# Products with the values in three batches per head pair of the first layer instead of six

## The reference, cut to what matters

```python
a1 = _attn(q, k1, v1, causal=True)
a2 = _attn(q, ks, vs, causal=False)
a3 = _attn(q, kw, vw, causal=True)
g = gate[:, :, None, None, None]
out = g[:, 0] * a1 + g[:, 1] * a2 + g[:, 2] * a3
out = out.transpose(0, 2, 1, 3).reshape(B, T, N_HEAD * V_HEAD)
return out @ w_proj
```

## Time and profile before

| | us |
|---|---|
| median of 3 runs (lowest, highest) | 3538.37 (3537.81, 3544.86) |
| the profiled execution's own time | 3538.17 |
| its span, first to last instruction | 3536.3 |
| busy: PE, PEld, DVE, ACT, POOL | 3216.3, 2335.8, 1985.7, 1558.5, 929.1 |
| mean granted clock of TensorE, share of full speed | 0.942 |
| matmuls of line 897 with the first layer's values / ones / 64 selected keys' values | 337.8 / 404.6 / 67.2 |

### The profile page before, as it was taken

One profiled execution on the slowest core, in us unless ns is written; L12 is line 12 of the kernel. 1 busy time (PEld: TensorE's weight loads), 2 busy tenths in 40 slices (PEclk: granted clock), 3 DMA queues, 4 the chain that ended last, 5 costly groups with the idle time before them and its releaser, 6 DMA issues. The chain is left out here.

```text
span 3536.3 us, 58809 instructions
## 1 busy us (share of the span) xinstructions
PE 3216.3 (91%) x20560; PEld 2335.8 (66%) x20560; DVE 1985.7 (56%) x6978; ACT 1558.5 (44%) x3441; POOL 929.1 (26%) x1840
## 2 busy tenths in 40 slices
PE   4999889997899979999889998899889997899988
PEld 3776657765677656776567765677656776577665
DVE  3665466646566465664656646566465654566545
ACT  1454345543455334553445535455253552545434
POOL 0222222222222222222222232222322223222222
PEclk8999899998899989999999998999989998999989
DMA  2000000000000000000000000100000000000000
GB/s 90 28 13 13 1 14 25 19 7 1 20 19 19 7 1 25 19 13 7 1 25 19 13 7 1 31 16 10 7 1 32 19 7 6 14 19 19 11 3 7
DMA packets 31438, 53.75 MB, mean 15 GB/s; under 512 B 3472, under 2 KB 13456, under 8 KB 30864
## 3 DMA queue, kind: packets, MB, share of 16 engines
q1 hardware_dynamic: 31120, 49.64, 4.4%
HBM read 44.91 MB, written 4.72 MB: 14 GB/s over the span
## 5 line engine op out<-in xcount | busy, mean ns | idle before, releaser
L1483 ACT ACTIVATE PR<-work 128x512 f32<-128x512 f32 (+1 forms) x1088 | 641.9, 599 | 574.6 <-PE work L860 472.3
L1125 DVE CUSTOM_DVE_ANT_0 work<-work,KEEPB 128x384 f32<-128x384 f32 (+3 forms) x1536 | 666.5, 481 | 75.9 <-PE work L821 74.6
L1609 POOL TENSOR_SCALAR_AFFINE_SELECT PR<-PR 128x256 f32<-128x256 f32 (+1 forms) x960 | 348.6, 367 | 925.9 <-ACT PR L1483 921.8
L821 PE MATMUL work<-BIG 96*128 96x448 f32 (+9 forms) x1664 | 446.2, 364 | 39.0 <-DVE NMX L1125 15.8
L1109 DVE TENSOR_TENSOR BIG<-work,BIG 96x512 fp32r<-96x512 f32 (+1 forms) x455 | 284.6, 628 | 326.9 <-ACT BIG L1378 325.9
L1599 POOL TENSOR_TENSOR TOK<-AB 128x256 f32<-128x256 f32 (+1 forms) x325 | 220.1, 677 | 850.2 <-DVE AB L1079 850.2
L858 PE MATMUL work<-BIG 99*128 99x512 f32 (+4 forms) x1152 | 404.5, 351 | 0.3
L897 PE MATMUL outs<-PR,ONES 128*32 128x512 f32 (+4 forms) x2304 | 404.6, 458 | 0.0
L821 PEld LDWEIGHTS work<-BIG 96*128 96x128 f32 (+1 forms) x1664 | 279.9, 203 | 184.1 <-issue 92.5
L859 PE MATMUL work<-BIG 96*128 96x512 f32 (+4 forms) x1152 | 382.6, 332 | 0.0
L860 PE MATMUL work<-BIG 96*128 96x512 f32 (+4 forms) x1152 | 381.7, 331 | 0.0
(11 more groups left out here) (163 smaller groups left out, 5291.6 us busy)
## 6 DMA issues: line engine op xcount, KB each, us to landing
WKW<-w_kw_dram SPq DMA_DIRECT2D x65, 256.0 KB, 2.7
WSEL<-w_sel_dram SPq DMA_DIRECT2D x65, 256.0 KB, 3.0
X<-x_dram SPq DMA_DIRECT2D x9, 512.0 KB, 3.4
out_dram<-X SPq DMA_DIRECT2D x9, 512.0 KB, 2.8
WFC<-w_fc_dram SPq DMA_DIRECT2D x1, 1024.0 KB, 9.6
WFP<-w_ffp_dram SPq DMA_DIRECT2D x1, 1024.0 KB, 11.6
WQKV<-w_qkv_dram SPq DMA_DIRECT2D x1, 768.0 KB, 12.8
WQ<-w_q_dram SPq DMA_DIRECT2D x1, 576.0 KB, 7.1
```

Source lines behind the costliest of these rows:

```text
L821: last = mm(ps[:, col:col + n], q, k, start=(i_mm == 0), stop=(i_mm == len(u["mm"]) - 1))
L1125: last = v.tensor_tensor_reduce(ps[:, lo:hi], ps[:, lo:hi], KEEPB[:, T - (hi - lo):T], -1.0, -NEG, ALU.add, ALU.min, dst)
L1483: a.activation(PR[0:rows, j % NP, :], ps[0:rows, :], ACT.Exp).then_inc(exp_ready, 1)
L1609: gp.affine_select(blocks, blocks, [[0, len(cols)], [1, P]], ALU.is_ge, 0.0, base=0, channel_multiplier=-1).then_inc(exp_masked, 1)
```

## The change

Units 4, 5 are now tile 2 of a1 and a3, units 6, 7 tile 0 of a3 and 8, 9 its tiles 1 and 3. A batch takes four units: the first a1's tiles 0, 1, 3, the second a1's tile 2 and a3's 0 and 2, the third a3's 1 and 3 and the selected keys. a1 is complete with the second batch, a3 and a2 with the third. The selected keys' products take all 128 rows: rows 64 to 127 of their slot hold older exponentials, which meet zeros in `VS` and in a second block of `ONES`. Where two attentions complete with one batch, the second's `out_tr` and `norm` are due 1.2 units later (0.4 in the last pair).

```diff
--- before.py
+++ after.py
@@ -86,8 +86,8 @@
 
 def units0():
     out = []
-    for what in ([(A1, 0, 0)], [(A1, 1, 0), (A1, 3, 384)], [(A3, 0, 0)], [(A3, 1, 0), (A3, 3, 384)],
-                 [(A1, 2, 0), (A3, 2, 256)], [(A2, 0, 0)]):
+    for what in ([(A1, 0, 0)], [(A1, 1, 0), (A1, 3, 384)], [(A1, 2, 0), (A3, 2, 256)],
+                 [(A3, 0, 0)], [(A3, 1, 0), (A3, 3, 384)], [(A2, 0, 0)]):
         for h in range(2):
             out.append([(a, h, j, col) for a, j, col in what])
     return out
@@ -114,12 +114,13 @@
 
 CAUSAL = [[i for i in range(NU[layer]) if diagonal(layer, i)] for layer in range(2)]
 MASK0 = [0, NPAIR * len(CAUSAL[0])]
-PV = [[(2 * k, 2 * k + 1) for k in range(6)], [(0, 1), (2, 3), (4,)]]
+PV = [[tuple(range(4 * k, 4 * k + 4)) for k in range(3)], [(0, 1), (2, 3), (4,)]]
 NPV = [len(k) for k in PV]
 UNIT0 = [0, NPAIR * NU[0]]
 PV0 = [0, NPAIR * NPV[0]]
 
-COMPLETE = [{4: [A1, A3], 5: [A2]}, {2: [0]}]
+LAST = [{A1: 2, A3: 3, A2: 0}, {0: 2}]
+COMPLETE = [{1: [A1], 2: [A3, A2]}, {2: [0]}]
 
 
 
@@ -168,15 +169,15 @@
         for k, units in enumerate(PV[layer]):
             t = t0 + units[-1] + o["pv"]
             at.append((t, ("pv", p, k)))
-            for a in COMPLETE[layer].get(k, []):
+            for late, a in enumerate(COMPLETE[layer].get(k, [])):
                 if layer == 0:
                     what, group = p, a == A2 and p % 2
                 elif p % 2:
                     what, group = p // 2, True
                 else:
                     continue
-                t1 = t + 0.3 + o["tr"]
-                at += [(t + 0.3, ("out", what, a)), (t1, ("out_tr", what, a)), (t1 + 0.1, ("norm", what, a))]
+                t1 = t + 0.3 + (0.4 if p == NPAIR - 1 else 1.2) * late + o["tr"]
+                at += [(t + 0.3 + 0.1 * late, ("out", what, a)), (t1, ("out_tr", what, a)), (t1 + 0.1, ("norm", what, a))]
                 if layer == 0 and a == A2:
                     at.append((t1 + 0.1 + o["sum"], ("sum", p)))
                 if group and layer == 0 and p == NPAIR - 1:
@@ -411,7 +412,7 @@
         COS1, SIN1 = sb("COS1", [P, NT, 8]), sb("SIN1", [P, NT, 16])
         ID = sb("ID", [P, P])
         KEEPB = sb("KEEPB", [P, T], BF16)
-        ONES = sb("ONES", [P, 32])
+        ONES = sb("ONES", [P, 2, 32])
         BEFB = sb("BEFB", [P, P], BF16)
         ONEB = sb("ONEB", [P, P], BF16)
         MEANW = sb("MEANW", [P, P])
@@ -443,7 +444,7 @@
         QZ = BIG[:, 0:8192].rearrange("p (g h k) -> p g h k", g=NPAIR, h=2)
         KB = BIG[:, 8192:12288].rearrange("p (g k) -> p g k", g=NPAIR)
         VV = sb("VV", [P, 3, NT, 2, 64])
-        VS = sb("VS", [KEEP, 3, 64])
+        VS = sb("VS", [P, 3, 64])
         TOK = sb("TOK", [P, 4, HG, D0])
         AB = sb("AB", [P, 2, 512])
         OH = AB[:, 1, 0:NT * KEEP].rearrange("p (t c) -> p t c", t=NT)
@@ -588,7 +589,7 @@
                       (WP[:, :, :], w_proj), (WFC[:, :, :], w_fc), (WFP[:, :, :], w_ffp), (WQKV[:, :, :], w_qkv),
                       (WO[:, :, :], w_o), (WSG[:, :, :], w_sign)]
         EARLY_LOADED, LATE_LOADED = 16 * len(early_loads), 16 * len(late_loads)
-        SET_UP = 16
+        SET_UP = 19
         THRESHOLDS = spike_thresholds()
         x_rows = x.rearrange("(n p) c -> p n c", p=P)
         out_rows = out.rearrange("(n p) c -> p n c", p=P)
@@ -867,13 +868,13 @@
 
 
                 units = PV[layer][k]
-                if units[-1] in CAUSAL[layer]:
-                    pe.wait_ge(exp_masked, MASK0[layer] + p * len(CAUSAL[layer]) + CAUSAL[layer].index(units[-1]) + 1)
-                else:
+                masked = [CAUSAL[layer].index(i) for i in units if i in CAUSAL[layer]]
+                pe.wait_ge(exp_masked, MASK0[layer] + p * len(CAUSAL[layer]) + masked[-1] + 1)
+                if units[-1] not in CAUSAL[layer]:
                     pe.wait_ge(exp_ready, UNIT0[layer] + p * NU[layer] + units[-1] + 1)
-                if layer == 0 and p and k in (0, 2, 5):
-
-                    pe.wait_ge(evacuated, 3 * (p - 1) + {0: A1, 2: A3, 5: A2}[k] + 1)
+                if layer == 0 and p:
+
+                    pe.wait_ge(evacuated, 3 * (p - 1) + [A1, A3, A2][k] + 1)
                 elif layer and k == 0:
                     pe.wait_ge(evacuated, 3 * NPAIR + max(p // 2 - 2, 0))
                 parts = [(i, part) for i in units for part in UNITS[layer][i]]
@@ -882,9 +883,8 @@
                 for n in range(0, len(parts), 2):
                     for side in range(2 - layer):
                         for i, (a, h, j, col) in parts[n:n + 2]:
-                            rows = KEEP if layer == 0 and a == A2 else P
                             if side:
-                                v = ONES[0:rows, :]
+                                v = ONES[:, int(a == A2), :]
                             elif layer == 1:
                                 v = VP[:, j, 2 * p + h, :]
                             elif a == A2:
@@ -894,8 +894,8 @@
                             bank = OB[a if layer == 0 else p // 2 % 3]
                             row = 64 * (p % 2 if layer else side) + 32 * h
                             slot = (UNIT0[layer] + p * NU[layer] + i) % NP
-                            last = mm(bank[row:row + 32, j * P:T], v, PR[0:rows, slot, col:col + T - j * P],
-                                      start=(j == 0), stop=(j == 2 or a == A2), skip_group_check=True)
+                            last = mm(bank[row:row + 32, j * P:T], v, PR[:, slot, col:col + T - j * P],
+                                      start=(j == 0), stop=(j == LAST[layer][a]), skip_group_check=True)
                 last.then_inc(pv_done, 1)
 
             def transpose_tiles(use, src):
@@ -1287,7 +1287,10 @@
             v.memset(MHALF[:, :], -0.5).then_inc(set_up, 1)
 
             v.tensor_scalar(WS[:, :, P:P + ROPE], WS[:, :, P:P + ROPE], 1.0 / H, None, ALU.mult).then_inc(set_up, 1)
-            v.memset(ONES[:, :], 1.0).then_inc(set_up, 1)
+            v.memset(ONES[:, 0, :], 1.0).then_inc(set_up, 1)
+            v.memset(ONES[0:KEEP, 1, :], 1.0).then_inc(set_up, 1)
+            v.memset(ONES[KEEP:P, 1, :], 0.0).then_inc(set_up, 1)
+            v.memset(VS[KEEP:P, :, :], 0.0).then_inc(set_up, 1)
             v.memset(CKVT[0:QL, :], 0.0).then_inc(set_up, 1)
             v.memset(SELT[:, :, KEEP:P], 0.0).then_inc(set_up, 1)
             for h in range(2):
@@ -1438,7 +1441,7 @@
                     if what == "qk":
                         read_work(copy(VV[:, p % NPAIR % 3, t, A3, :], ps[:, 384:448]), use)
                     else:
-                        read_work(copy(VS[:, p % NPAIR % 3, :], ps[0:KEEP, 192:256]), use)
+                        read_work(copy(VS[0:KEEP, p % NPAIR % 3, :], ps[0:KEEP, 192:256]), use)
 
             def high_parts(p, m):
 
@@ -1460,7 +1463,7 @@
             def outputs(layer, n, att):
 
                 if layer == 0:
-                    act.wait_ge(pv_done, PV0[0] + n * NPV[0] + (6 if att == A2 else 5))
+                    act.wait_ge(pv_done, PV0[0] + n * NPV[0] + (2 if att == A1 else 3))
                     if n:
                         full(act, (0, "out_tr", n - 1, att), WORK)
                     copy(OE[0][:, att, :], OB[att][:, :]).then_inc(evacuated, 1)
```

## The result

The changed kernel takes 3597.19 us (median of 4 runs, 3592.08 to 3598.36) against 3538.64 for the kernel before (3537.81 to 3544.86) beside it: ratio 1.0159, 95% interval 1.0141 to 1.0176. It is slower by 58.6 us, where 24 were forecast, and 10 us above the upper end of the forecast's range, 3587.

The account below looks back on a forecast made before the run. PE's instruction order was taken to bound the kernel; -6.5 us for fewer batches plus waits of 5.25, 2.8, 0.3 and 1.2 gave +3.05 us per pass, +24.4 in all: 3562 us, range 3496 to 3587 (forecast's own 3546 to 3587).

Parts of the forecast that it names:

- wait A: PE before the next pair's first maxima, until ACT copies and DVE subtracts the last piece: 0.75 us, seven places per pass.
- wait B: PE at the ninth unit, until DVE has read the seventh maximum from its bank: about 0.4 us, seven places per pass.
- wait C: First output's normalisation precedes the next piece's rotary products on DVE, delaying a later piece's bank: 0.3 us per pass.
- wait D: PE at the end of a pass, around the last batch and the output transposes behind it: 1.2 us per pass.
- term 3: New order of units within a pair: the same units run per pair, so no cost.
- Term 1: Six batches per pair become three, each edge pair worth 0.27 us: 6.5 us less per pass, 51.8 us in all.
- Term 4: The wait ahead of a pair's first maxima, behind ACT's chain of eight copies: 5.25 us per pass.
- Term 5: The wait among the maxima, where the ninth unit needs the seventh maximum's bank: 2.8 us per pass.
- Term 7: End of pass: 0.8 us idle PE behind the last batch, 0.4 us waiting for its last exponentials, 1.2 us together.
- Term 6: A piece's bank wait behind the first output's normalisation on DVE: 0.05 us for each of six pairs, 0.3 per pass.
- R1: Rival: the copies keep up, so the kernel gets faster: 3496 us (chance 0.12), or 3526 us with half the waits (0.22).
- R3: Rival: a batch's edge pair is worth only 0.11 us instead of 0.27, giving 3593 us; chance 0.06.

Follow-up runs that it names:

- the last runs: Changed kernel with copies, outputs, first batch moved and last two transposed pieces ahead of the fourth unit: 3528.59 us; last pair's batch cut too: 3521.33 us.

## Why the prediction was right in direction and short in size

| us per pass | forecast | measured |
|---|---|---|
| 1 fewer edges | -6.5 | -6.8 |
| 2, 3 zero rows, unit order | 0 | 0 (zero rows: run alone) |
| 4 wait A | +5.25 (7 places of 0.75) | +6.2 (6 places of 1.03) |
| 5 wait B, 7 places | +2.8 | +4.5 (4 of 0.58, 3 of 0.72) |
| 6 wait C | +0.3 | 0 |
| 7 wait D | +1.2 | +1.17 (0.36 + 0.81) |
| first pair of a pass | a seventh place of wait A | +1.1 |
| sum | +3.05 | +6.2 (in all: +7.1) |

The 0.9 us between the sum and the whole are in none of the terms; about half of it are matmuls that step 0.08 us slower right behind wait A. The order of the units (term 3) was not run by itself.

**Term 1** held to 5%. It was read off one batch of one width, and the batches of mixed widths cost about the same on average.

**Term 4** was mis-sized, 1.03 us a place instead of 0.75. "The small one behind it ... ending at about T + 5.2" was exact (5.18). What failed is the step after it: I let PE start when DVE's record ends, but it starts 0.25 us later (1495.65 to 1495.90, and so in 52 of the trace's 56 places; 0.26 in the run with the copies moved). I also did not see that the unit ahead waits as well; since the maxima start at T + 5.43 either way, that split cost nothing more. In the earlier trace rows the maxima start at 1501.78 and DVE had ended at 1501.50: no wait of PE stood in the trace of before from which the restart could be read, and I treated it as nothing where it should have been a bound of its own. Seen from the 0.25 us, PE had 0.03 us to spare there.

**Term 5** was mis-sized too, 0.65 instead of 0.4, for other reasons. In a pair without a group the account of DVE held: it starts the fourth maximum 0.51 behind PE and is through with the seventh 3.54 us after PE's start of the fourth (forecast 3.63 to 3.73), and PE starts the ninth unit 0.06 us later (1472.06 to 1472.12). But PE would have been there after 3.13 us, not 3.25, and the first matmul behind the wait steps 0.29 us instead of 0.18: 0.58. In the three pairs with a group the step that failed is "the ninth unit (index 8) takes the bank of the seventh maximum": the group's transposes stand between the two there, the unit takes their bank, and it starts 0.05 us after ACT's copy of it (1503.96 to 1504.01): 0.72. The forecast had looked at a pair without a group and does not name this copy. The two terms, with the first pair, are 3.75 us per pass, 30 of the 34 us that were missing.

**Left out: the first pair.** Term 4 has "seven places", but only six of a pass's first maxima have the last batch of a pair before them. In the first pair of a pass there is none, but its own first batch went from ahead of the maxima to behind them, and PE waits 0.37 + 1.29 us there instead of 0.54: +1.1 per pass, 9 us in all. No run put that batch back ahead of the maxima, so this cause is argued. The change moves that batch too, and a place without the usual neighbour should have been looked at by itself.

**Term 7** was right in both its parts, and the cut of the last pair took away the 0.81, of which 0.30 came back. **Term 6** was nothing.

**The rivals.** R1 fell: the copies do not keep up in the order given. That PE can be kept busy with the same copies in another order is what the last runs show, so the low busy shares of ACT and DVE did speak truly of throughput, only not of latency. R3 fell by the split batch; beside the estimate of 0.107 us the prediction says "the row shows twice that", where 0.27 is 2.5 times as much. The rule of "TensorEngine Tiling", "PSUM Bottleneck" in the Trainium skill, agrees in sign: of fewer batches' gain of 55 us nothing was left. But it speaks of the copies' rate. At 101 us of 200 for ACT the rate was not short; what cost the time were a chain and a latency without cover.

The upper end of the range, 3587, had A 0.9 and B 0.55 at the most. Both terms came out above the bounds that I had drawn from rows without any wait in them.

## What to carry to other kernels

A batch that one merges away was also cover for somebody's latency. Before merging, list for each gap the latency from the last producer through every engine to the consumer, restart included, and put other work behind the last producer rather than ahead of it. Moving work out of a gap where PE waits costs its full length elsewhere, and look apart at the first and last turn of a loop, whose neighbours differ.

## What the runs showed of the hardware

- A waiting PE started its maxima 0.25 us after the end of the DVE record that released it, in 52 of 56 places. A unit that waited for a bank started 0.05 or 0.06 us after one (1493.79 + 0.69 to 1494.53, 1472.06 to 1472.12). The unit has one semaphore wait, the first maxima have eight (seven pieces and the bank), and between the end of DVE's record (1495.65) and the start of PE (1495.90) the trace has two more semaphore instructions of PE's queue, at 1495.69 and 1495.80. That they make the difference is likely; no run left them out.
- Of 48 waits of 1.4 us, 16 were followed 2 us later by some 3 us at half clock with PE busy all the while, which made the pair 1.6 us longer; of the waits of 1.05 us, or of 0.49 and 0.55 a unit apart, none was. The first pair's wait of 1.29 us was in 2 of 8 passes of the run with the copies moved, and in none of the changed kernel's.
- Switching a batch on and off in 32-column tiles cost 0.27 to 0.28 us per pair of edges over all batches removed, and 0.32 in the period of a pair where one was added. These are averages over batches of 128 to 512 columns.
